# Half products, softmax pieces and masks: a graph network's node pass on one core

## What is computed

```python
att = einsum('mhd,mhd->mh', Q[receivers], K[senders]) / sqrt(32)
e = exp(att - segment_max(att, receivers)[receivers])
attention = e / segment_sum(e, receivers)[receivers]
out = segment_sum(attention[:, :, None] * V[senders], receivers) @ W_ff.T + b_ff
x = layernorm(x + out)
out = concat([x, segment_sum(msgs, receivers)], axis=1) @ W_comb + b_comb
x = layernorm(x + out)
```

## Time and profile before

| | us |
|---|---|
| median of 3 runs (1093.03 to 1094.83) | 1093.58 |
| the profiled execution | 1091.44 |
| its span, first to last instruction | 1089.8 |
| PE busy | 1029.4 (94%) |
| DVE busy | 940.5 (86%) |
| POOL busy | 873.6 (80%) |
| ACT busy | 844.0 (77%) |

### The profile page before, as it was taken

The page is one execution under the profiler, slowest core; times in us unless marked ns, Lnnn a source line. Parts: engine busy times, 40 slices in busy tenths (PEclk is TensorE's granted clock), DMA queues, the critical chain, the costliest instruction groups (busy, mean ns, idle before and its releaser), DMA issues.

```text
span 1089.8 us, 26087 instructions
## 1 busy us (share of the span) xinstructions
PE 1029.4 (94%) x7400; PEld 972.2 (89%) x7400; DVE 940.5 (86%) x2645; ACT 844.0 (77%) x2550; POOL 873.6 (80%) x705
## 2 busy tenths in 40 slices
PE   5889999999999999999979799989999999999994
PEld 4779999999999999999868687878999999999993
DVE  5879888898888988889999889758999999999992
ACT  3877777777777777777768788887888888888883
POOL 5588888888888888888788888946888888888884
PEclk9999999999999999999989899998999999999997
DMA  4876666666666666666546456856666666766741
GB/s 157 303 260 223 231 236 231 236 231 231 220 234 227 229 231 231 233 225 219 189 148 219 156 200 238 301 192 180 176 188 192 199 196 199 199 199 200 201 139 43
DMA packets 121390, 227.29 MB, mean 209 GB/s; under 512 B 33587, under 2 KB 61486, under 8 KB 121184
## 3 DMA queue, kind: packets, MB, share of 16 engines
q1 hardware_dynamic: 104000, 189.54, 52.9%
q0 software_dynamic: 17248, 36.08, 10.4%
HBM read 137.84 MB, written 93.59 MB: 212 GB/s over the span
## 4 chain that ended last, share of the span: by engine, by line
PE 82%; DVE 7%; issue 5%; ACT 3%; SPq 2%; DMA 1%; DVEq 0%; POOL 0%; ACTq 0%; POOLq 0%
PE ps L992 8%; PE ps L865 7%; PE ps L844 6%; PE ps L904 5%; PE ps L905 4%; PE ps L906 4%; PE ps L858 4%; PE ps L859 4%; PE ps L860 4%; PE ps L1031 4%; PE ps L1002 2%; PE ps L1004 2%; PE ps L926 2%; PE ps L1003 2%; PE ps L972 2%
## 5 line engine op out<-in xcount | busy, mean ns | idle before, releaser
L688 POOL TENSOR_TENSOR zin<-xin,bff_row 128x1024 f32<-128x1024 f32 x98 | 233.4, 2382 | 31.9 <-DVE stat L1446 13.9
L1474 DVE SCALAR_TENSOR_TENSOR yn<-ps,r,bc 128x256 f32<-128x256 f32 x391 | 169.2, 474 | 60.8 <-PE ps L860 37.4
L865 PE MATMUL ps<-w_mix,zT 128*128 128x256 f32 x780 | 189.1, 393 | 8.0 <-DVE yn L1474 4.5
L865 PEld LDWEIGHTS ps<-w_mix,zT 128*128 128x128 f32 x780 | 147.7, 197 | 31.6 <-ACT zT L1111 8.0
L1126 ACT ACTIVATE junk<-yn 128x256 f32<-128x256 f32 x391 | 157.8, 415 | 9.5 <-DVE yn L1474 9.2
L1446 DVE BATCH_NORM_STATS2 stat<-zin 128x6 f32<-128x256 f32 x391 | 135.4, 408 | 1.9 <-issue 1.6
L730 POOL DMA_INDIRECT ty<-in_node_type_dram,src_i x98 | 103.9, 1061 | 25.7 <-issue 23.7
L742 POOL DMA_INDIRECT xs<-in_x_dram,idx x98 | 93.8, 957 | 29.6 <-issue 29.6
L766 POOL DMA_INDIRECT out_dram<-oe,idx x98 | 97.9, 999 | 24.0 <-issue 20.2
L858 PE MATMUL ps<-mix_hi,z_hi 128*128 128x256 f32 x392 | 114.2, 291 | 3.0 <-DVE z_lo L1511 3.0
L844 PE MATMUL ps<-ident,xin 128*128 128x128 f32 (+1 forms) x782 | 106.8, 282 | 8.9 <-DMA xin<-in_x_dram 8.9
(11 more groups left out here) (220 smaller groups left out, 3589.7 us busy)
## 6 DMA issues: line engine op xcount, KB each, us to landing
xin<-in_x_dram SPq DMA_DIRECT2D x97, 512.0 KB, 4.0
out_dram<-on SPq DMA_DIRECT2D x97, 512.0 KB, 3.1
xd_o<-xdT SPq DMA_DIRECT2D x49, 256.0 KB
v_o<-vT SPq DMA_DIRECT2D x49, 256.0 KB, 2.2
v<-v_o SPq DMA_DIRECT2D x49, 256.0 KB, 2.6
xd<-xd_o SPq DMA_DIRECT2D x49, 256.0 KB
abc<-a_o SPq DMA_DIRECT2D x196, 64.0 KB, 2.6
sbc<-same_o SPq DMA_DIRECT2D x49, 128.0 KB, 3.1
```

The lines of the kernel that those rows point to most:

```text
L688: pool.tensor_tensor(z, xx, bb, ALU.add).then_inc(n_z, 1)
L865: last = mm(ps[0:np_, half(g, j), (j % 2) * D:(j % 2 + 1) * D], zT[:, g % 2, k, j * P:j * P + np_], w_mix[:, k, :], start=k == 0, stop=k = ...
L1474: last = dve.scalar_tensor_tensor(out=yn[0:np_, q, j * D:(j + 1) * D], in0=ps[0:np_, half(g, j), (j % 2) * D:(j % 2 + 1) * D], scalar=r1[0 ...
```

## The change

PE's softmax pieces move from the head of the step to its end, behind `z_product(g, 1)`; their step numbers stay. DVE's k = -2, 0, 1, 2 and 3 move from steps 56 and 58 to 61 into the edge-block steps 31, 35, 39, 43 and 47 (blocks 22, 26, 30, 34 and 38). For this the masks' tiles are placed behind those that the edge blocks use: `under_edges` is a spacer of 7 D columns, `kr` is dropped and `rest` grows by what `kr` had. The last two masks also sum their mask into `mask_sum`, which nobody reads; that gives them the accumulating form of the operation.

```diff
--- before.py
+++ after.py
@@ -204,8 +204,10 @@
     def sx(name, shape, dt=F32):
         return softmax.enter_context(nc.sbuf_tensor(name, shape, dt))
 
-    same_c, next_c, first_c, last_c, neg_a, neg_b = (sx(n, [RC, CH]) for n in ("same_c", "next_c", "first_c", "last_c", "neg_a", "neg_b"))
-    run_c, seg_c, ex_c, a_c = (sx(n, [RC, CH]) for n in ("run_c", "seg_c", "ex_c", "a_c"))
+    neg_a, neg_b, run_c, seg_c, ex_c, a_c = (sx(n, [RC, CH]) for n in ("neg_a", "neg_b", "run_c", "seg_c", "ex_c", "a_c"))
+    under_edges = sx("under_edges", [RC, 7 * D])
+    same_c, next_c, first_c, last_c = (sx(n, [RC, CH]) for n in ("same_c", "next_c", "first_c", "last_c"))
+    mask_sum = sx("mask_sum", [RC, 2])
     softmax.close()
 
     last_pass = ExitStack()
@@ -233,9 +235,9 @@
     ze_hi, ze_lo = (z_hi[:, :, c, :].rearrange("p a (c n) -> p a c n", c=2) for c in range(DC))
     num_hi, num_lo = (z_lo[:, :, c, :].rearrange("p a (c n) -> p a c n", c=2) for c in range(DC))
     xdT, vT = (sb(n, [P, 2, 2, EB]) for n in ("xdT", "vT"))
-    qr, kr = (sb(n, [P, 2, EB]) for n in ("qr", "kr"))
+    qr = sb("qr", [P, 2, EB])
     prod = sb("prod", [P, 2 * D])
-    rest = sb("rest", [P, 13 * D])
+    rest = sb("rest", [P, 15 * D])
 
 
     s_w = sem("weights_landed")
@@ -1043,20 +1045,6 @@
         pe.wait_ge(s_wready, 2)
         for g in range(G):
             b = g - LEAD
-            if g == AFTER + 1:
-                score_chunks()
-            if g == AFTER + 4:
-                chunk_ends(0)
-            if g == AFTER + 7:
-                chunk_ends(1)
-            if g == AFTER + 9:
-                carry_columns(0)
-            if g == AFTER + 16:
-                chunk_ends(2)
-            if g == AFTER + 18:
-                carry_columns(1)
-            if g == AFTER + 33:
-                type_transposes()
             if b == 0:
                 pe.wait_ge(s_wtc, 6)
                 pe.wait_ge(s_wlo, 6)
@@ -1075,6 +1063,20 @@
                 k_product(b)
                 v_product(b)
             z_product(g, 1)
+            if g == AFTER + 1:
+                score_chunks()
+            if g == AFTER + 4:
+                chunk_ends(0)
+            if g == AFTER + 7:
+                chunk_ends(1)
+            if g == AFTER + 9:
+                carry_columns(0)
+            if g == AFTER + 16:
+                chunk_ends(2)
+            if g == AFTER + 18:
+                carry_columns(1)
+            if g == AFTER + 33:
+                type_transposes()
 
         pe.wait_ge(c_out, 16)
         pe.wait_ge(c_same, 16 * NCH)
@@ -1572,6 +1574,8 @@
             dve.tensor_copy(carry[:, n, :], ps[0:RC, C, 3 * P:3 * P + 2]).then_inc(c_step, 1)
             dve.wait_ge(c_step, step["sum_columns" if n else "maximum_columns"])
 
+        MASKS = {22: -2, 26: 0, 30: 1, 34: 2, 38: 3}
+
         def softmax_step(k):
 
             if k == -2:
@@ -1583,13 +1587,13 @@
             elif k == 1:
                 dve.tensor_tensor(next_c[:], dcf[:, 1:CH + 1], dcf[:, 2:CH + 2], ALU.is_equal).then_inc(c_mask, 1)
             elif k == 2:
-                dve.tensor_scalar(first_c[:], dcf[:, 1:CH + 1], dcf[:, 1:2], None, ALU.is_equal).then_inc(c_mask, 1)
+                dve.tensor_scalar(first_c[:], dcf[:, 1:CH + 1], dcf[:, 1:2], None, ALU.is_equal, ALU.add, accum_out=mask_sum[:, 0:1]).then_inc(c_mask, 1)
                 dve.wait_ge(c_mask, 3)
                 dve.tensor_copy(flags[:, 0:1], same_c[:, 0:1]).then_inc(c_step, 1)
                 dve.tensor_copy(flags[:, 1:2], first_c[:, CH - 1:CH]).then_inc(c_step, 1)
                 dve.tensor_copy(flags[:, 2:3], next_c[:, CH - 1:CH]).then_inc(c_step, 1)
             elif k == 3:
-                dve.tensor_scalar(last_c[:], dcf[:, 1:CH + 1], dcf[:, CH:CH + 1], None, ALU.is_equal).then_inc(c_mask, 1)
+                dve.tensor_scalar(last_c[:], dcf[:, 1:CH + 1], dcf[:, CH:CH + 1], None, ALU.is_equal, ALU.add, accum_out=mask_sum[:, 1:2]).then_inc(c_mask, 1)
             elif k == 4:
                 dve.wait_ge(c_neg, 1)
                 dve.wait_ge(c_att, 1)
@@ -1758,7 +1762,10 @@
                     dve.tensor_tensor(mix_lo[:, k, :], w_mix[:, k, :], mix_hi[:, k, :], ALU.subtract).then_inc(s_mix, 1)
             if g == LEAD + 30:
                 table_parts()
-            softmax_step(g - AFTER)
+            if g - LEAD in MASKS:
+                softmax_step(MASKS[g - LEAD])
+            if g >= AFTER + 4:
+                softmax_step(g - AFTER)
         rstd2(G - 2)
         y(G - 1, 1)
         rstd2(G - 1)
```

## The result

The changed kernel takes **1087.21 us** in the median of four executions (1086.60 to 1088.04), beside 1093.30 us (1093.01 to 1094.83) of the kernel before: ratio 0.9942 [0.9925, 0.9959]. The profiled execution took 1088.04 us (span 1086.4). The forecast was 1077.0 us with a range of 1071.5 to 1083.0: the sign was right, the time lies 4 us outside the range.

A forecast was written before the change was run, and what follows sets the result against it. DVE was taken to pace steps 58 to 83, with DVE and PE holding each other up; 5.5 + 10.7 + 2 - 1.8 = 16.4 us off the profiled 1091.44 gave 1075.0, against the median 1077.0 us, range 1071.5 to 1083.0.

The forecast's parts named there:

- The masks leave steps 58 to 61: Softmax stage: without its four masks (10.3 us of DVE), DVE's step 62 begins earlier, a gain of 5.5 us.
- PE's pieces: Steps 62 to 83: pieces behind the second half product end DVE's waits for PE, a gain of 10.7 us (low end 7).
- The port: DVE's later softmax operations waiting for POOL's port: the largest waits shrink, a gain of 2 us, bounds -4 to +5.
- The masks among the edge blocks: Edge blocks: mask work that doesn't fit DVE's gaps delays PE, a cost of 1.8 us, ends -0.5 and -4.5.
- None of it meets POOL's addition if that keeps its place: Edge blocks: moved masks avoid POOL's addition, which in step 43 starts 0.9 us after DVE's gap closes.
- The rival "slower": Edge blocks: three operations each wait for POOL's whole addition and PE's clock falls; 1095.7 us, chance 0.03.
- POOL becomes the pace: Softmax stage: gathers stretched beside DVE's two-input operations leave POOL 5 us short; gain 11.4, 1082.2 us, chance 0.13.

The follow-up runs named there:

- 1: Kernel before with only PE's pieces moved behind the second half product; masks back in steps 58 to 61 in old forms: 1088.58 us, ratio 0.9932.
- 5: Changed kernel with POOL's addition held behind DVE's softmax operations in the stage, and behind conversion, masks and table parts among the edge blocks: 1075.85 us, ratio 0.9836.
- 9: Kernel before with PE's pieces moved, masks in steps 58 to 61, POOL's addition held behind DVE's softmax operations and the table parts: 1076.83 us, ratio 0.9840.
- 4: Changed kernel with POOL's addition in the softmax stage held until DVE's softmax operation of the step before is done: 1081.71 us, ratio 0.9883.
- 10: Changed kernel with DVE's `far` operation in step 65 in the accumulating form, POOL unchanged: 1088.62 us, ratio 0.9950.
- 6: Kernel before with PE's pieces moved, masks in steps 58 to 61, POOL's addition held behind DVE's softmax operations, masks included: 1077.97 us, ratio 0.9858.
- 7: Kernel before with only POOL's addition held behind DVE's softmax operation of the step before, masks included: 1083.75 us, ratio 0.9913.
- 8: Kernel before with only POOL's addition of step 40 held until DVE's table parts of step 39 are done: 1090.36 us, ratio 0.9968.
- 2: Kernel before with only the masks moved to the edge blocks; PE's pieces at the head of their steps: 1094.28 us, ratio 0.9999.
- 3: Changed kernel with the receivers' conversion in step 31 in the accumulating form: 1087.88 us, ratio 0.9930.

## Why the prediction was wrong, step by step

**The masks leave steps 58 to 61: 5.5, right where it was measured.** DVE's step 62 begins 18.38 us behind the first half product of step 58 (549.76 - 531.38) instead of 23.72: 5.34 us. Of that 4.0 are left at the end of the stage (137.2 beside 141.2 of 1), and with POOL held back 1.2 (5 beside 9): most of what the masks cost there was waiting for POOL, not their own work.

**PE's pieces: 10.7, right as to the waits, too high as a gain.** The waits went as described. But in 1, which has this part alone, the stage gained 7.2 us. DVE's softmax operations from step 62 on sum to 42.30 us in the kernel before, to 46.62 in 1: a DVE that no longer waits for PE meets a POOL that waits less for DVE (from 549 us on 9.4 us instead of 16.3). I counted a wait that ends as a gain, though the next resource was already taken.

**The port: +2, the step that failed first.** It came out at about -6: the softmax operations sum to 47.98 us instead of 42.30, outside the bounds of -4 to +5. I had argued that POOL's shifts no longer wait for masks and so POOL runs further behind DVE. What happened is in the POOL rows: with fewer waits for DVE, POOL's gather, scaling and addition follow each other without a gap, and DVE's operation waits for as many of the last two as are in line. Before, the gaps in which POOL waited for DVE were DVE's chance. 4 bears it out: with POOL held behind DVE's softmax operation, 41.39 us. The Trainium skill (SBUF — State Buffer, Who interferes with whom) states that whichever of the two issues first gets the shared pair for its whole instruction and the other fully blocks; `same_c` at 323.19 agrees, which ends 0.96 us behind an addition that began 1.06 us ahead of it. The profile's starts don't always tell who was first: in 1 the table parts' operation starts at 358.82 and loses to an addition that starts at 359.44. What happens to the blocked one when the holder has its next instruction ready, the runs show: in `far` and in `lr` of 10, DVE got in neither behind the gather nor behind the scaling.

**The masks among the edge blocks: -1.8, the second step that failed.** The profile shows -7.9; with POOL held back, -1.6 (5). Of the 7.9, a third to a half is chance, the execution that it is measured against: one that pays the table parts' wait loses 2.6 to 4.1 us there with no mask (1, 6 and 7). By 5, the masks' excess was sized rightly in sum (and the accumulating form exactly, 1.14), and what failed is the sentence "None of it meets POOL's addition if that keeps its place". I had read the place in one step, 43, where the addition starts 0.9 us behind DVE's gap, and had left out that an operation issued during the gather ahead of it can lose to the addition as well. In the changed kernel's profiled execution the conversion does so at once, DVE slips by 2.6 us, and every later operation has another phase. The rival "slower" had this mechanism, but asked for three whole additions and a fallen clock each time; the granted clock stayed at 1.00 behind the first two waits (283 to 300 and 320 to 335 us) and was 0.89 only from 360 to 375 us.

**POOL becomes the pace** is refuted by 4, 5 and 7: POOL is given waits and the time falls. I had kept it because a gather had grown to 1.64 us beside a two-input operation; its price took a stretch of 1.2 us for each gather, where these rows give 0.69. The Trainium skill's inference (SBUF — State Buffer, Who interferes with whom), that such an operation takes only the read interface and leaves descriptor generation alone, would have ruled the rival out, though the gather of 1.64 us doesn't fit it. In the other direction the `cr` rows fit: tensor_tensors ran beside a gather with nothing lined up behind it. By these rows, the 3.31 us in 1 are the addition's and not the gather's.

**The sum.** In the profiled executions 11.1 - 7.9 = 3.2 of the 3.4 us are accounted for. The medians differ by 6.1, and 1 and 8 suggest why: the usual execution of the kernel before pays the table parts' wait, and the one I read did not. The range's lower end doesn't follow from its terms: 5.5 + 10.7 + 5 - 0.5 off 1093.58 is 1072.9 and not 1071.5.

## What to carry to other kernels

Where two engines share a port, time taken from one engine's waits can be handed to the other's queue: look at whether the freed engine's operations now follow each other without a gap, because then the other's single operation waits for all of them. A phase read in one step is no bound for an operation in another; where two operations stand a few tenths of a microsecond apart, price both orders. The cheap remedy was a semaphore that lets the engine with slack go second (10 us in 7), and it was worth more than moving the masks (nothing that the runs can tell in 2 and in 5 beside 9).

## What the hardware showed that I had not expected

- An operation of DVE that waits for the port doesn't get it when POOL's operation ends, if POOL's next is ready: 3.76 us for 448 numbers (after), 4.06 us for a scan of 112 (10).
- A tensor_tensor of DVE issued 0.35 us behind the start of POOL's indirect gather waited for the addition lined up behind the gather (3.31 instead of 0.43 us, 1), and so did a conversion from int32 to f32 issued 0.33 us behind it (3.54 us in the changed kernel, 0.62 in 5). Issued 0.11 and 0.30 us behind the start, a tensor_tensor and the conversion didn't wait (1.09 and 0.63 us, 2). With nothing lined up, two tensor_tensors issued 0.46 us behind it took 0.55 us (2.04 with the scaling lined up, 4). The 0.90 us of the conversion before was partly a wait.
- The accumulating form never waited: 1.14, 1.15, 1.08 and 0.58 us in after, 3 and 10, with POOL busy beside it.
- A shift of 0.45 us between two engines at the end of one step (0.10 us ahead of a gather in the kernel before, 0.35 behind its start in 1) decides over a wait whose removal moved the kernel's median by 3.5 us (8).
